# Messages in 25 tiles of 128 nodes, one P add in four on VectorE, key one-hots on ScalarE, and the second update ahead in the last stage of a two-layer graph network

## The chip, the cores and the metric

The kernel runs on 1 core of one Trainium2 chip. The metric is the device time of one execution in microseconds (us). Short names for the engines are those of the profile: PE (TensorE, with PEld for its weight loads), DVE (VectorE), ACT (ScalarE), POOL (GpSimd) and SP (SyncE, which only issues transfers).

## The reference, cut to what matters

There are 3,125 nodes with 256 features and 50,000 edges sorted by their destination. Layer 0 is a max-pooling graph layer. Layer 1, which this change touches, is an attention layer:

```python
h = relu(layernorm(x))
e = edge_emb[edge_type]                       # 16 types
messages = (h[src] + e) @ msg_W + msg_b
att_in = concat([h[src], h[dst], e, task_rep])
edge_delta = tanh(gelu(att_in @ att_W1 + att_b1) @ att_W2 + att_b2)
edge_weight = 1.0 + edge_scale * edge_delta
messages = (messages * (1 + 0.5 * tanh(msg_gamma)) + msg_beta) * edge_weight
agg = segment_sum(messages, dst) / max(segment_sum(edge_weight, dst), 1)
agg = agg * (1 + 0.5 * tanh(upd_gamma)) + upd_beta
updated = gelu(concat([h, agg]) @ up_W1 + up_b1) @ up_W2 + up_b2
y = h + updated
x = x + layernorm(y) * ln_g + ln_b
```

## The kernel before

The nodes are cut into 28 windows of 112 (WIN), taken four at a time (GN = 4) as 7 node groups (NG). The edges, sorted by destination, are put into 418 slots of up to 128 edges, so that a slot's destinations lie in one window; four slots (SG) are one edge group, which gives 105 edge groups (NGR), the last with 2 slots. The program has three parts that matter here; all orders are written out by hand, engine by engine, with semaphores between the engines.

**Node stage.** For each node group PE turns the rows of h (`turn_h`, L1397), DVE copies the result from PSUM into `up` (L1709), and `messages` (L1409) multiplies it by two weight matrices of 256 columns each. That gives per node a row of 512 numbers: P (256, the source's part of the attention input) and M (256, the message without edge weight). One message tile is the 112 nodes of one window, with 4 matmuls; ACT and DVE take turns in copying it out (`take`), and SP writes it to `pm_d` in HBM. `neigh` (L1386) and `keys_q` (L1422) are other products of the same stage; `keys_q` makes Q, the destination's part, which is kept in three bf16 pieces in `qw`.

**Edge stage.** `edge_step(g)` is run by every engine for each edge group g. POOL gathers the rows [P, M] of the four slots from `pm_d` (L1353), six groups of buffers round. PE (L1490, L1492) builds z of a slot in PSUM: three bf16 matmuls with the key one-hot `hot` (which edge belongs to which node of the window, and to which type) as weights and the three pieces of Q as data, and one fp32 matmul with the identity that adds the gathered P. Slots 0 and 1 lie in one PSUM bank, 2 and 3 in the next, and groups take turns between two pairs of banks. ACT applies Gelu to each bank (L1596). DVE multiplies by the attention vector and sums to a logit (L1763). One step later ACT makes the edge weight from it (tanh L1608, scale L1610) and scales the placement one-hots `place` (L1615); two steps after z PE sums the messages with them into windows (L1516, banks 4 to 7), and three steps after z DVE adds these sums into `acc` (L1750). DVE also makes the one-hots: types and placement (L1753, L1754), and the keys of the group after (`match_keys(g + 1)`, L1727). `hot` has two buffers. In 9 of the 105 groups (`pair_of`) PE also multiplies a pair of windows by the first half of `up_W1` (L1503), and ACT puts the result back into `up` (L1602).

**Last stage.** Per node group: ACT makes a diagonal of 1/degree, PE multiplies the aggregates with it (`update`, L1874), DVE adds the node's own part (`update`, L1956), ACT applies Gelu (L1935), PE multiplies by `up_W2` (`rows_y`, L1884), DVE adds h and takes the statistics (`rows_y`, L1966 to L1977), POOL takes the root (L1847), DVE makes the shift (`shifts`, L1982), ACT normalizes (L1922), and DVE multiplies and adds (`put`, L1990, L1993). PE's `update(i)` waits until DVE has read what `update(i - 1)` left in the bank:

```python
for f in range(2):
    if i >= 1:
        eng.wait_ge(u_ready, 2 * i - 1 + f)
```

Of the kernel before, what the change touches and what calls it, by code (L numbers as in the profile page):

```python
# [6 lines left out]
def gnn_two_layers(nc, A, out):  # L7
# [8 lines left out]
    P = 128  # L16
# [60 lines left out]
    with top:  # L77
# [1072 lines left out]
        with b34:  # L1150
# [12 lines left out]
            pm = [gbuf[0:WIN, r * GN * 2 * D:(r + 1) * GN * 2 * D] for r in range(2)]  # L1163
# [8 lines left out]
            onec = cols[:, 0:1]  # L1172
            ramp = bank(7)[:, AW:AW + P]
# [41 lines left out]
            hot_ready = sem("hot_ready")  # L1215
            z_ready = sem("z_ready")
            gelu_ready = sem("gelu_ready")
# [48 lines left out]
            def pm_parts(i):  # L1266
                return [(0, GN)] if i < NG - 1 else [(0, 2), (2, 3), (3, 4)]
# [7 lines left out]
            def _(eng):  # L1275
# [6 lines left out]
                for i in range(NG):  # L1282
# [3 lines left out]
                    for k0, k1 in pm_parts(i):  # L1286
                        eng.wait_ge(pm_a, 2 * i + (k1 + 1) // 2)
                        eng.wait_ge(pm_v, 2 * i + k1 // 2)
                        rows = slice((i * GN + k0) * WIN, (i * GN + k1) * WIN)
                        eng.dma_start(pm_d[rows, :].rearrange("(k p) d -> p k d", p=WIN), rows_by_k(pm[i % 2])[:, k0:k1, :])\  # L1290
                           .then_inc(pm_out[i % 2], 16)
# [66 lines left out]
            def _(eng):  # L1358
# [31 lines left out]
                def turn_h(i):  # L1390
                    eng.wait_ge(h_ready, i + 1)
                    if i >= 1:
                        eng.wait_ge(pm_a, 2 * i - 1)
                        eng.wait_ge(pm_v, 2 * i - 1)
# [18 lines left out]
                def keys_q(i):  # L1413
# [5 lines left out]
                    for k in range(GN):  # L1419
                        at = (i * GN + k) * ACW0  # L1420
                        for hf in range(2):
                            ins = eng.matmul(q_bank(i)[0:WIN, k * D:(k + 1) * D], up[:, at + hf * WIN:at + (hf + 1) * WIN],  # L1422
# [24 lines left out]
                for i in range(NG):  # L1447
# [5 lines left out]
                    messages(i, range(GN))  # L1453
# [5 lines left out]
                def own_early(p):  # L1459
                    if p == 0:  # L1460
                        eng.wait_ge(pm_a, 2 * NG)
                        eng.wait_ge(pm_v, 2 * NG)
                    if p >= 3:
                        eng.wait_ge(u_out, p - 2)
                    for f in range(2):
                        for hf in range(2):
                            ins = eng.matmul(early_bank(p)[:, f * ACW0:(f + 1) * ACW0], upw1[:, hf * D + f * P:hf * D + (f + 1) * P],
                                             pair_cols(p)[:, :, hf, :], start=hf == 0, stop=hf == 1)
# [10 lines left out]
                def edge_step(g, r, n):  # L1479
                    if has(g):  # L1480
# [17 lines left out]
                    if p is not None:  # L1498
                        eng.wait_ge(logit_ready, g)
                        for f in range(2):  # L1500
                            to = bank(2 * ((g + 1) % 2))[:, f * ACW0:(f + 1) * ACW0]
                            for hf in range(2):
                                ins = eng.matmul(to, upw1[:, hf * D + f * P:hf * D + (f + 1) * P],  # L1503
                                                 pair_cols(p)[:, :, hf, :], start=hf == 0, stop=hf == 1)
                        ins.then_inc(u_ready, 1)
                    if has(g - 2):
# [16 lines left out]
            def _(eng):  # L1523
# [16 lines left out]
                def take(i, k):  # L1540
                    if k == 0 and i >= 2:
                        eng.wait_ge(pm_out[i % 2], 16 * (i // 2))
                    eng.wait_ge(pm_ready, GN * i + k + 1)
                    eng.activation(pm[i % 2][:, k * 2 * D:(k + 1) * 2 * D], bank(4 + k)[0:WIN, :], ACT.Copy).then_inc(pm_a, 1)
# [486 lines left out]
```

## Time and profile before

| | us |
|---|---|
| median of 3 runs (1302.63 to 1306.84) | 1305.84 |
| the profiled execution's own time | 1307.77 |
| its span, from the first to the last instruction | 1305.8 |
| PE busy, share of the span | 937.8 (72%) |
| DVE busy | 899.9 (69%) |
| POOL busy | 831.5 (64%) |
| ACT busy | 605.0 (46%) |

The span contains both layers. The node stage begins near 551 us, PE's first matmul of the edge stage is at 700.65 us, and the last stage begins at 1230.8 us. A share of the whole span is a mean over stages with different limits, so each stage has to be read by itself, from the rows of its own stretch of time.

### The profile page before, as it was taken

To read this page: it belongs to the slowest core of one execution; us is meant where nothing else is said; L and a number is where in the kernel's file an instruction comes from. 1 tells how busy PE (TensorE), PEld (TensorE's weight loads), DVE (VectorE), ACT (ScalarE), POOL (GpSimd) and SP (SyncE) were. 2 spreads that over 40 slices of the span, in tenths; PEclk is the share of its full clock that TensorE was granted. 3 is DMA by queue.
4 is the path that set the end of the run, shared out by engine and by line. 5 is a ranking of instruction groups with operands and counts; after the bars stand their busy time and mean duration, and the time that the engine had idled before them with its cause. 6 is when DMAs were issued, how large, how long until landed. Compare 5 with 4: busy or idle time off the path is not lost. (4 is left out here: it accounts for less than half of the span.)

```text
span 1305.8 us, 18685 instructions
## 1 busy us (share of the span) xinstructions
PE 937.8 (72%) x5019; PEld 728.9 (56%) x5019; DVE 899.9 (69%) x2594; ACT 605.0 (46%) x1479; POOL 831.5 (64%) x868
## 2 busy tenths in 40 slices
PE   7505455664123511389899999999999999999985
PEld 6402233332112510277677777777777777777774
DVE  6477575665566544345656888888888888888658
ACT  6433333433243433223325665566666656556544
POOL 0377777777777777663127777777777777777012
PEclk9855555555555555589899999999999999999988
DMA  5568666566776666544357777877877787887312
GB/s 157 133 201 279 220 214 216 201 224 221 241 261 232 201 204 216 191 116 130 69 152 231 235 234 235 241 235 234 238 239 236 232 236 241 234 235 237 99 38 85
DMA packets 100774, 263.58 MB, mean 202 GB/s; under 512 B 21094, under 2 KB 42117, under 8 KB 94530
## 3 DMA queue, kind: packets, MB, share of 16 engines
q0 software_dynamic: 53856, 164.87, 42.7%
q1 hardware_dynamic: 45026, 95.76, 22.1%
q10 hardware_dynamic: 1792, 1.75, 0.5%
q8 instruction: 46, 0.75, 0.2%
q14 instruction: 54, 0.44, 0.1%
HBM read 192.92 MB, written 68.25 MB: 200 GB/s over the span
## 5 line engine op out<-in xcount | busy, mean ns | idle before, releaser
L675 POOL DMA_INDIRECT gath<-hp_d,chain_src x391 | 370.8, 948 | 169.3 <-issue 166.3
L1353 POOL DMA_INDIRECT gbuf<-pm_d,srcs x350 | 332.1, 949 | 108.5 <-issue 104.1
L922 DVE SCALAR_TENSOR_TENSOR hist<-hist,smask,ps 128x256 f32<-128x256 f32 x390 | 186.7, 479 | 194.8 <-ACT ps L716 186.8
L716 ACT ACTIVATE ps<-gath,chain_w 128x256 f32<-128x256 f32 x391 | 164.6, 464 | 312.9 <-DMA gath<-hp_d,chain_src 295.1
L1750 DVE TENSOR_TENSOR acc<-ps,acc 112x272 f32 x418 | 183.7, 439 | 69.2 <-DVE acc L1750 64.0
L1596 ACT ACTIVATE ps<-ps 128x512 f32<-128x512 f32 x210 | 122.1, 582 | 191.7 <-PE ps L1492 191.6
L1492 PE MATMUL ps<-gbuf,ident 128*128 128x256 f32 x700 | 210.1, 382 | 0.0
L1490 PE MATMUL ps<-qw,halves 128*128 x1254 | 206.6, 274 | 2.3 <-DVE qw L1699 2.3
L1516 PE MATMUL ps<-gbuf,placed 128*112 128x272 f32 x700 | 175.4, 393 | 1.0 <-ACT placed L1615 0.7
L837 PE MATMUL ps<-win_hot,node_hot 128*112 128x28 bf16 x391 | 43.7, 253 | 175.2 <-DVE win_hot L1009 175.2
L1490 PEld LDWEIGHTS ps<-qw,halves 128*128 128x128 bf16 x1254 | 122.9, 98 | 73.8 <-issue 6.9
L1516 PEld LDWEIGHTS ps<-gbuf,placed 128*112 128x112 f32 x700 | 123.4, 177 | 35.2 <-ACT placed L1615 1.2
L837 PEld LDWEIGHTS ps<-win_hot,node_hot 128*112 128x112 bf16 x391 | 40.0, 207 | 181.2 <-DVE win_hot L1009 179.8
L1763 DVE CUSTOM_DVE_ANT_0 gbuf<-ps,w2b 128x256 f32<-128x256 f32 x350 | 127.6, 417 | 8.6 <-ACT ps L1596 8.6
L1615 ACT ACTIVATE placed<-placed,logit 128x112 f32<-128x112 f32 x418 | 128.0, 376 | 3.4
L1492 PEld LDWEIGHTS ps<-gbuf,ident 128*128 128x128 f32 x700 | 106.4, 192 | 3.9
L761 PE MATMUL ps<-wsT,hT_s 128*112 128x256 f32 x112 | 57.2, 666 | 50.7 <-ACT hT_s L723 40.4
L1353 POOL DMA_INDIRECT attw<-pm_d,srcs x68 | 64.3, 946 | 21.1 <-issue 20.4
L761 PEld LDWEIGHTS ps<-wsT,hT_s 128*112 128x112 f32 x112 | 30.1, 299 | 71.8 <-issue 54.9
L1754 DVE TENSOR_TENSOR placed<-ps,edgef 128x448 f32<-128x448 f32 x105 | 64.4, 613 | 0.0
L1847 POOL TENSOR_TENSOR rs_c<-ve_c,power 112x4 f32<-112x4 f32 x7 | 12.5, 1789 | 77.1 <-DVE ve_c L1977 77.1
L1007 DVE TENSOR_TENSOR node_hot<-ps,low 128x896 bf16<-128x896 f32 (+1 forms) x49 | 52.9, 1080 | 0.0
(292 smaller groups left out, 1384.2 us busy)
## 6 DMA issues: line engine op xcount, KB each, us to landing
hist_d<-hist SPq DMA_DIRECT2D x48, 1024.0 KB, 4.6
gath<-hp_d,chain_src POOLq DMA_INDIRECT x391, 3.1
wn<-node_row_d SPq DMA_DIRECT2D x26, 224.0 KB
key<-node_row_d SPq DMA_DIRECT2D x26, 224.0 KB, 3.5
gbuf<-pm_d,srcs POOLq DMA_INDIRECT x350, 4.0
pm_d<-gbuf SPq DMA_DIRECT2D x6, 896.0 KB, 5.1
hb_d<-gbuf SPq DMA_DIRECT2D x7, 448.0 KB, 3.2
qw<-hb_d SPq DMA_DIRECT2D x7, 448.0 KB, 8.4
```

Source lines behind the costliest of these rows:

```text
L675: eng.indirect_dma_start(row_at(j), None, hp_d[:, :], bass.IndirectOffsetOnAxis(ap=chain_src[:, j:j + 1], axis=0)).then_inc(got[q % RINGG] ...
L716: eng.activation(weighted_at(j), row_at(j), ACT.Copy, scale=chain_w[:, j:j + 1]).then_inc(gw_ready, 1)
L761: ins = eng.matmul(bank(6, 2)[0:WIN, k * D:(k + 1) * D], hT[i % 2][:, (k * 2 + hf) * WIN:(k * 2 + hf + 1) * WIN], wsT[:, hf * D:(hf + 1) * ...
L922: eng.scalar_tensor_tensor(out=state_at(j), in0=state_at(j - 1) if j else first_state[:, :], scalar=smask[:, j:j + 1], in1=weighted_at(j), ...
L1353: eng.indirect_dma_start(gath3(g % RING)[:, k, 0:2 * D], None, pm_d[:, :], bass.IndirectOffsetOnAxis(ap=srcs[:, g * SG + k:g * SG + k + 1] ...
L1490: eng.matmul(to, hot[g % 2][:, k * P:(k + 1) * P], qw[:, bass.ds(w[k] * (3 * D) + part * D, D)], start=part == 0, stop=False)
L1492: ins = eng.matmul(to, ident[:, :], gath3(r)[:, k, 0:D], start=False, stop=True)
L1516: eng.matmul(bank(4 + k)[0:WIN, 0:AW], place[q % 3][:, k * WIN:(k + 1) * WIN], gath3(q)[:, k, D:SW], start=True, stop=True).then_inc(sums_ ...
L1596: eng.activation(zb, zb, ACT.Gelu).then_inc(gelu_ready, 1)
L1615: ins = eng.activation(at, at, ACT.Copy, scale=logit[q][:, k:k + 1])
L1750: eng.tensor_tensor(to, bank(4 + k)[0:WIN, 0:AW], to, ALU.add).then_inc(summed, 1)
L1763: ins = eng.tensor_tensor_reduce(gath3(r)[:, k, 0:D], zk, w2b[:, :], 1.0, 0.0, ALU.mult, ALU.add, logit[r % 3][:, k:k + 1])
```

## The change

Four edits, in one file:

1. Message tiles are 128 nodes wide: 25 tiles (the last of 64 nodes) instead of 28 of 112. For this `up` is laid out as two halves of 3,136 columns, so that 128 neighbouring nodes are neighbouring columns; DVE's copy of the turned rows is two instructions of 128x448 instead of one of 128x896. A node group completes 3, 4, 3, 4, 3, 4 and 4 tiles.
2. For the fourth slot of each full edge group PE leaves out the fp32 matmul with the identity, and DVE adds P into PSUM (semaphore `p_added`). ACT's second Gelu of the group waits for it.
3. `match_keys` moves from DVE to ACT and becomes two passes: |key - p| in place with ACT's Abs and the bias `less` = -p, then relu(1 - that) into `hot`. PE's wait for `hot_ready` ahead of the fourth placement matmul is dropped.
4. In the last stage DVE runs `update(1)` ahead of `rows_y(0)` and `shifts(0)`.

```diff
-            def pair_cols(p):
-                return up[:, p * 2 * ACW0:(p + 1) * 2 * ACW0].rearrange("p (k h n) -> p k h n", k=2, h=2)
+            def nodes(n0, n1, half):
+                return up[:, half * NT * WIN + n0:half * NT * WIN + n1]
+
+            def pair_cols(p, half):
+                return nodes(p * 2 * WIN, (p + 1) * 2 * WIN, half).rearrange("p (k n) -> p k n", k=2)
...
+            def tiles_of(i):
+                first, last = i * GN * WIN // P, (i + 1) * GN * WIN // P
+                return range(first, last if i < NG - 1 else -(-NM // P))
+
+            def nodes_in(m):
+                return min(P, NM - m * P)
...
+            def p_by_vector(g, k):
+                return slots_in(g) == SG and k == SG - 1
...
-                def messages(i, ks):
...
-                    for k in ks:
-                        if i >= 1 and k >= 2:
-                            eng.wait_ge(pm_a if k == 2 else pm_v, 2 * i)
-                        at = (i * GN + k) * ACW0
+                    for k, m in enumerate(tiles_of(i)):
+                        if i >= 1 and k == 2:
+                            eng.wait_ge(pm_a, by_act(i))
+                        if i >= 1 and k == 3:
+                            eng.wait_ge(pm_v, by_vec(i))
+                        n = nodes_in(m)
                         for half, w in enumerate((attw[:, 0:2 * D], mc[:, :])):
                             for hf in range(2):
-                                ins = eng.matmul(bank(4 + k)[0:WIN, half * D:(half + 1) * D], up[:, at + hf * WIN:at + (hf + 1) * WIN],
+                                ins = eng.matmul(bank(4 + k)[0:n, half * D:(half + 1) * D], nodes(m * P, m * P + n, hf),
                                                  w[:, hf * D:(hf + 1) * D], start=hf == 0, stop=hf == 1)
                         ins.then_inc(pm_ready, 1)
...
                         for k in range(slots_in(g)):
                             to = bank(2 * (g % 2), 2)[:, k * D:(k + 1) * D]
                             for part in range(3):
-                                eng.matmul(to, hot[g % 2][:, k * P:(k + 1) * P],
-                                           qw[:, bass.ds(w[k] * (3 * D) + part * D, D)], start=part == 0, stop=False)
-                            ins = eng.matmul(to, ident[:, :], gath3(r)[:, k, 0:D], start=False, stop=True)
+                                ins = eng.matmul(to, hot[g % 2][:, k * P:(k + 1) * P],
+                                           qw[:, bass.ds(w[k] * (3 * D) + part * D, D)], start=part == 0,
+                                           stop=part == 2 and p_by_vector(g, k))
+                            if not p_by_vector(g, k):
+                                ins = eng.matmul(to, ident[:, :], gath3(r)[:, k, 0:D], start=False, stop=True)
                             if k == slots_in(g) - 1:
                                 ins.then_inc(z_ready, 2 - k // 2)
...
                             if k == SG - 1:
                                 eng.wait_ge(match_ready, min(g + 1, NGR))
-                                eng.wait_ge(hot_ready, min(g + 2, NGR))
                             eng.matmul(bank(4 + k)[0:WIN, 0:AW], place[q % 3][:, k * WIN:(k + 1) * WIN],
...
+                eng.wait_ge(one_set, 2)
+
+                def match_keys(g):
+                    n, at = g // KG, g % KG * GW
+                    key_g = key[n % 2][:, at:at + GW]
+                    eng.wait_ge(key_in[n % 2], (n // 2 + 1) * 32)
+                    eng.activation(key_g, key_g, ACT.Abs, bias=less[:, 0:1]).then_inc(apart, 1)
+                    eng.wait_ge(apart, g + 1)
+                    eng.activation(hot[g % 2], key_g, ACT.Relu, scale=-1.0, bias=onec).then_inc(hot_ready, 1)
+
+                match_keys(0)
...
                 def edge_step(g, r, n):
                     if has(g):
                         for half in range(2):
                             eng.wait_ge(z_ready, g * 2 + half + 1)
+                            if half == 1 and slots_in(g) == SG:
+                                eng.wait_ge(p_added, g + 1)
                             zb = bank(2 * (g % 2) + half)
                             eng.activation(zb, zb, ACT.Gelu).then_inc(gelu_ready, 1)
+                    if has(g + 1):
+                        match_keys(g + 1)
...
                     eng.wait_ge(t_ready, i + 1)
-                    eng.tensor_copy(up[:, i * GN * ACW0:(i + 1) * GN * ACW0].rearrange("p (k c) -> p k c", k=GN),
-                                    bank(4, 2).rearrange("p (k c) -> p k c", k=GN)[:, :, 0:ACW0]).then_inc(hT_ready, 1)
+                    for hf in range(2):
+                        ins = eng.tensor_copy(nodes(i * GN * WIN, (i + 1) * GN * WIN, hf).rearrange("p (k n) -> p k n", k=GN),
+                                              bank(4, 2).rearrange("p (k c) -> p k c", k=GN)[:, :, hf * WIN:(hf + 1) * WIN])
+                    ins.then_inc(hT_ready, 1)
...
-                    if has(g + 1):
-                        match_keys(g + 1)
+                    if has(g) and slots_in(g) == SG:
+                        eng.wait_ge(z_ready, g * 2 + 2)
+                        zk = bank(2 * (g % 2), 2)[:, (SG - 1) * D:SG * D]
+                        eng.tensor_tensor(zk, zk, gath3(r)[:, SG - 1, 0:D], ALU.add).then_inc(p_added, 1)
...
                 update(0)
+                update(1)
                 rows_y(0)
                 shifts(0)
-                update(1)
```

On ACT, the second edge group in the loop, before (L1596 Gelu, L1608 and L1610 the edge weight of the group before, L1615 its placement one-hots):

```order
L1596 ACTIVATE ps<-ps 128x512 [waits z_ready] x2
L1608 ACTIVATE logit1<-logit1,b2c 128x4 [waits logit_ready]
L1610 ACTIVATE logit1<-logit1,cols,esc 128x4 [waits delta_ready]
L1615 ACTIVATE placed<-placed,logit1 128x112 [waits match_ready,ew_ready]
L1615 ACTIVATE placed<-placed,logit1 128x112 x3
```

The same group's rows after the change (L1639 Gelu, L1624 Abs, L1626 Relu, which gives `hot_ready`):

```order
L1639 ACTIVATE ps<-ps 128x512 [waits z_ready]
L1639 ACTIVATE ps<-ps 128x512 [waits p_added,z_ready]
L1624 ACTIVATE key<-key,less 128x512 [waits key_in1]
L1626 ACTIVATE halves<-key,cols 128x512 [waits apart]
L1653 ACTIVATE logit1<-logit1,b2c 128x4 [waits logit_ready]
L1655 ACTIVATE logit1<-logit1,cols,esc 128x4 [waits delta_ready]
L1660 ACTIVATE placed<-placed,logit1 128x112 [waits match_ready,ew_ready]
L1660 ACTIVATE placed<-placed,logit1 128x112 x3
```

The keys of group g + 1 stand behind the second Gelu of group g, and that Gelu now waits for DVE as well as for PE.

On DVE, one edge group before, from the one-hots to the logits (L1753, L1754 types and placement, L1727 keys, L1763 logits):

```order
L1753 TENSOR_TENSOR gbuf<-ps,edgef 128x4x16
L1754 TENSOR_TENSOR placed<-ps,edgef 128x448
L1727 TENSOR_TENSOR halves<-key,ps 128x512 [waits key_in1]
L1763 ISA gbuf,logit1<-ps,w2b 128x256 [waits gelu_ready]
L1763 ISA logit1 128x1
```

After (L1798, L1799 types and placement, L1804 the P add, L1810 logits):

```order
L1798 TENSOR_TENSOR gbuf<-ps,edgef 128x4x16
L1799 TENSOR_TENSOR placed<-ps,edgef 128x448
L1804 TENSOR_TENSOR ps<-ps,gbuf 128x256 [waits z_ready]
L1810 ISA gbuf,logit0<-ps,w2b 128x256 [waits gelu_ready]
L1810 ISA logit0 128x1
```

The keys are gone from between the one-hots and the logits, and the P add, which waits until PE has made the whole group's z, stands in their place.

On DVE, the start of the last stage before (L1956 `update`, L1966 `rows_y`, L1982 `shifts`; semaphore names are shared with an earlier block):

```order
L1956 TENSOR_TENSOR u0<-ps,up 128x448 [waits x_in5] x2
L1966 TENSOR_TENSOR y_c0<-ps,qw 112x1024 [waits bias_in,hb_in0]
...
L1982 SCALAR_TENSOR_TENSOR nb_c<-mv_c,rs_c 112x4 [waits io_read]
L1956 TENSOR_TENSOR u1<-ps,up 128x448 [waits x_in5] x2
L1956 TENSOR_TENSOR u0<-ps,up 128x448 [waits x_in5,bias_in]
```

After (L2003 `update`, L2013 `rows_y`, L2029 `shifts`):

```order
L2003 TENSOR_TENSOR u0<-ps,up 128x448 [waits wp_in] x2
L2003 TENSOR_TENSOR u1<-ps,up 128x448 [waits wp_in] x2
L2013 TENSOR_TENSOR y_c0<-ps,qw 112x1024 [waits io_set,hb_in0]
...
L2029 SCALAR_TENSOR_TENSOR nb_c<-mv_c,rs_c 112x4 [waits wT_ready]
L2003 TENSOR_TENSOR u0<-ps,up 128x448 [waits wp_in,io_set]
```

The two adds of `update(1)` (u1) have moved ahead of the statistics of the first group.

## Rows read from the trace of the kernel before

**Rows 1.** Busy time by engine, edge stage: from, to, length, engines, clock, DMA.
```profile
700.65:1220.35 519.70, 519.70 (x2969) 405.57 (x2970) 443.51 (x1545) 313.76 (x842) 382.91 (x406) 1.00 0.78 232
```

**Rows 2.** Timeline of PE in one edge group: start, us, instruction, count.
```profile
904.91 0.49 PE L1490 MATMUL ps<-qw,halves 128*128 x3
905.24 0.60 PE L1492 MATMUL ps<-attw,ident 128*128 128x256 f32 x2
...
907.20 0.49 PE L1490 MATMUL ps<-qw,halves 128*128 x3
...
907.96 2.00 PE L1516 MATMUL ps<-gbuf,placed 128*112 128x272 f32 x8
...
909.79 0.49 PE L1490 MATMUL ps<-qw,halves 128*128 x3
```

**Rows 3.** Timeline of ACT in the same edge group.
```profile
908.16 0.58 ACT L1596 ACTIVATE ps<-ps 128x512 f32<-128x512 f32 x1 [0.94 <-PE ps L1492]
...
908.65 0.29 ACT L1608 ACTIVATE logit<-logit,b2c 128x4 f32<-128x4 f32 x1
...
908.98 0.39 ACT L1610 ACTIVATE logit<-logit,cols,esc 128x4 f32<-128x4 f32 x1
...
909.40 1.22 ACT L1615 ACTIVATE placed<-placed,logit 128x112 f32<-128x112 f32 x4
```

**Rows 4.** Timeline of DVE in the same edge group.
```profile
904.59 0.44 DVE L1750 TENSOR_TENSOR acc<-ps,acc 112x272 f32 x1
...
907.03 0.61 DVE L1754 TENSOR_TENSOR placed<-ps,edgef 128x448 f32<-128x448 f32 x1
907.56 0.68 DVE L1727 TENSOR_TENSOR halves<-key,ps 128x512 bf16<-128x512 bf16 x1
...
908.16 0.41 DVE L1763 CUSTOM_DVE_ANT_0 attw<-ps,w2b 128x256 f32<-128x256 f32 x1
...
909.53 0.43 DVE L1750 TENSOR_TENSOR acc<-ps,acc 112x272 f32 x1
```

**Rows 5.** ACT's groups by line and shape: busy us, mean ns, idle before.
```profile
L1608 ACT ACTIVATE logit<-logit,b2c 128x4 f32<-128x4 f32 x105 | 30.3, 288 | 0.0
...
L246 ACT ACTIVATE sd<-ve 112x4 f32<-112x4 f32 x7 | 1.4, 194 | 3.0 <-DVE ve L345 2.9
...
L269 ACT ACTIVATE hpo<-hpb 112x512 f32<-112x512 f32 x2 | 1.3, 629 | 1.1 <-DVE hpb L370 1.0
```

**Rows 6.** POOL's gathers in the edge stage, timeline.
```profile
905.47 0.94 POOL L1353 DMA_INDIRECT gbuf<-pm_d,srcs  x1 [0.30 <-issue]
```

**Rows 7.** Timeline of the node stage, message tiles of two node groups.
```profile
643.94 2.05 PE L1409 MATMUL ps<-attw,up 128*112 128x256 f32 x4 [1.67 <-DVE up L1709]
...
658.16 1.09 DVE L1709 COPY up<-ps 128x896 f32<-128x896 f32 x1 [3.53 <-PE ps L1397]
...
659.30 1.12 PE L1409 MATMUL ps<-attw,up 128*112 128x256 f32 x4 [1.19 <-DVE up L1709]
```

**Rows 8.** The chain that ended last, in the last stage, in order of time.
```profile
1241.86 3.47 PE ps L1884 x16
...
1249.87 0.16 DVE nb_c L1982
1250.03 0.55 DVE u L1956
...
1250.71 3.73 PE ps L1874 x16
...
1260.29 1.24 DVE y_c L1966
...
1266.72 2.01 PE ps L1874 x16
1268.73 0.89 PE ps L1862 x8
1269.62 3.12 PE ps L1884 x15
```

More of the change, by code:

```diff
@@ L1162, in gnn_two_layers @@
             gath = [gbuf[:, r * SG * SW:(r + 1) * SG * SW] for r in range(RING - 1)] + [attw[:, :]]
-            pm = [gbuf[0:WIN, r * GN * 2 * D:(r + 1) * GN * 2 * D] for r in range(2)]
+            pm = [gbuf[:, r * GN * 2 * D:(r + 1) * GN * 2 * D] for r in range(2)]
             h, hb, ngb = ([gbuf[0:WIN, (4 + 2 * n + r) * GN * D:(5 + 2 * n + r) * GN * D] for r in range(2)] for n in range(3))
@@ L1172, in gnn_two_layers @@
             onec = cols[:, 0:1]
+            less = s("less", [P, 1], fp32)
             ramp = bank(7)[:, AW:AW + P]
@@ L1238, in early_bank, with by_act, by_vec @@
                 return bank(4 + p % 3)
-            def pair_cols(p):
-                return up[:, p * 2 * ACW0:(p + 1) * 2 * ACW0].rearrange("p (k h n) -> p k h n", k=2, h=2)
+            def nodes(n0, n1, half):
+                return up[:, half * NT * WIN + n0:half * NT * WIN + n1]
+            def pair_cols(p, half):
+                return nodes(p * 2 * WIN, (p + 1) * 2 * WIN, half).rearrange("p (k n) -> p k n", k=2)
+            NM = NT * WIN
+            def tiles_of(i):
[3 more added lines that the diff above has]
+                return min(P, NM - m * P)
+            def by_act(i):
+                return sum((len(tiles_of(n)) + 1) // 2 for n in range(i))
+            def by_vec(i):
+                return sum(len(tiles_of(n)) // 2 for n in range(i))
             def slots_in(g):
                 return min(SG, USED - g * SG)
+            def p_by_vector(g, k):
+                return slots_in(g) == SG and k == SG - 1
             def gath3(r):
@@ L1266, in pm_parts @@
             def pm_parts(i):
-                return [(0, GN)] if i < NG - 1 else [(0, 2), (2, 3), (3, 4)]
+                return [(0, len(tiles_of(i)))] if i < NG - 1 else [(0, 2), (2, 3), (3, 4)]
+            assert len(tiles_of(NG - 1)) == GN and max(len(tiles_of(i)) for i in range(NG)) <= GN
             def put_all(eng):
@@ L1286, in _ @@
                     for k0, k1 in pm_parts(i):
[L1287 to L1291, printed above, removed]
+                        eng.wait_ge(pm_a, by_act(i) + (k1 + 1) // 2)
+                        eng.wait_ge(pm_v, by_vec(i) + k1 // 2)
+                        m0, m1 = tiles_of(i)[k0], tiles_of(i)[k1 - 1] + 1
+                        n = nodes_in(m1 - 1)
+                        eng.dma_start(pm_d[m0 * P:(m1 - 1) * P + n, :].rearrange("(k p) d -> p k d", p=n),
+                                      rows_by_k(pm[i % 2])[0:n, k0:k1, :]).then_inc(pm_out[i % 2], 16)
                     if i == REC_AT:
@@ L1452, in _ @@
                         turn_n(i + 2)
-                    messages(i, range(GN))
+                    messages(i)
                     if i + 2 < NG:
@@ L1467, in own_early @@
                             ins = eng.matmul(early_bank(p)[:, f * ACW0:(f + 1) * ACW0], upw1[:, hf * D + f * P:hf * D + (f + 1) * P],
-                                             pair_cols(p)[:, :, hf, :], start=hf == 0, stop=hf == 1)
+                                             pair_cols(p, hf), start=hf == 0, stop=hf == 1)
                     ins.then_inc(u_ready, 1)
@@ L1503, in edge_step @@
                                 ins = eng.matmul(to, upw1[:, hf * D + f * P:hf * D + (f + 1) * P],
-                                                 pair_cols(p)[:, :, hf, :], start=hf == 0, stop=hf == 1)
+                                                 pair_cols(p, hf), start=hf == 0, stop=hf == 1)
                         ins.then_inc(u_ready, 1)
@@ L1542, in take @@
                         eng.wait_ge(pm_out[i % 2], 16 * (i // 2))
-                    eng.wait_ge(pm_ready, GN * i + k + 1)
-                    eng.activation(pm[i % 2][:, k * 2 * D:(k + 1) * 2 * D], bank(4 + k)[0:WIN, :], ACT.Copy).then_inc(pm_a, 1)
+                    m = tiles_of(i)[k]
+                    n = nodes_in(m)
+                    eng.wait_ge(pm_ready, m + 1)
+                    eng.activation(pm[i % 2][0:n, k * 2 * D:(k + 1) * 2 * D], bank(4 + k)[0:n, :], ACT.Copy).then_inc(pm_a, 1)
                 def q_high(i):
@@ L1621, in _ @@
                 eng.memset(onec, 1.0).then_inc(one_set, 1)
+                eng.tensor_scalar(less[:, :], pcol[:, 0:1], -1.0, None, ALU.mult).then_inc(one_set, 1)
                 def merge():
```

47 lines of the change are left out of this document (23 added, 24 removed).

## The prediction

> **What bounds the kernel now.** I cut the span into stages with the view of busy time by stretches, and the edge stage is 519.7 of 1305.8 us [rows 1]. In it PE is busy all the time at full clock (2.4 GHz), DVE 443.5 us, ACT 313.8 us. So this is where most of the change acts, and I read one edge group there in the timeline, engine by engine.
>
> PE's group starts at 904.91 and the next at 909.79: 4.88 us [rows 2]. Four slots of z take the first part: a slot is three bf16 matmuls (0.33 to the start of the fp32 one) and the fp32 P matmul; from 904.91 to 907.20 are three slots, 0.763 each, so the P matmul is 0.43. The four placement matmuls with their split passes take from 907.96 to 909.79, 1.83. Nothing is left over: 4 x 0.763 + 1.83 = 4.88.
>
> Two other engines are close behind. DVE starts its first accumulation at 904.59 and the next group's at 909.53, 4.94, with no long idle [rows 4]. POOL needs 0.94 + 0.31 = 1.25 for a gather, 5.0 for the four of a group [rows 6]; it stays in step because its ring was filled ahead and because PE has extra matmuls in 9 groups. So a PE that needs less than 4.88 would gain little by itself: POOL's 418 gathers at 1.25 are 522 us, as long as the stage.
>
> In the last stage the chain of waits shows a hole: PE's `rows_y(0)` ends at 1241.86 + 3.47 = 1245.33, and its next matmul starts at 1250.71, because it waits for DVE's `update(1)`, which stands behind the statistics and the shift of group 0 [rows 8].
>
> **The change, part by part.**
>
> *P add and keys together.* PE's own work per group falls by the P matmul to 4.45. But two things that were independent are now in series. Before, the keys of group g + 1 were made by DVE ahead of the logits of group g, while PE was still in z(g). After, they stand on ACT behind the second Gelu of g, that Gelu waits for DVE's P add, and the P add waits for the last z of g. PE can't start z(g + 1) without these keys. Buffers don't help, since the maker of the keys never gets more than one group ahead. The loop, counted from PE's first matmul of z(g):
>
> - to the end of the last bf16 trio and the hand-over to DVE: 907.20 - 904.91 = 2.29, + 0.49 + 0.03 = 2.81 [rows 2]. (The 0.03 is the distance at which Gelu follows in the same way: 907.20 + 0.33 + 0.60 of the P matmuls = 908.13, Gelu at 908.16 [rows 3].)
> - P add, 128x256 from PSUM: not in the trace. Nearest are the accumulation of 112x272 from PSUM at 0.44 and the multiply of 128x256 at 0.41 [rows 4]; I take 0.42, plus 0.03 hand-over: 3.26.
> - second Gelu until the next ACT instruction can start: 908.16 to 908.65, 0.49 [rows 3]: 3.75.
> - Abs of 128x512 with a bias column. ACT on 512 columns without such an operand takes 0.629; a bias column adds 0.288 - 0.194 = 0.09 (tanh of 4 columns with it against the root of 4 columns without) [rows 5]. So 0.72, and a dependent ACT instruction starts 0.04 after its source ends (908.65 + 0.29 to 908.98) [rows 3]: 4.51.
> - Relu of the same size, also with a bias column: 0.72: 5.23.
> - hand-over to PE: 0.13 lie between the end of DVE's u (1250.03 + 0.55) and PE's matmul at 1250.71 [rows 8]; here a register instruction stands between, so I take 0.2: 5.43.
>
> Group time 5.43 against 4.88 is +0.55. There are 105 groups, so 104 steps from one to the next, 9 of them with the pair's matmuls; in those PE is busy with the pair while ACT makes the keys, and I count them as even. 95 x 0.55 = **+52 us**. The others have room in 5.43: ACT has 2 x 0.49 for Gelu, 0.65 + 0.76 for the keys, 0.33 + 0.42 + 1.22 for weights and placement [rows 3], 4.36 in all; DVE 4.94 - 0.60 (keys, 907.56 to 908.16) + 0.35 + about 0.1 of waiting for Gelu, 4.8 [rows 4]; POOL 5.0.
>
> The bounds. An Abs or Relu can't be shorter than the Gelu of the same size, 0.58 [rows 3]: loop 5.15, +26. bf16 input on ACT isn't in the trace. Upwards, two passes of 0.77 and 0.3 for the hand-over give 5.63, +71. The middle value is nearest to its rows, since only a pointer operand is added to the 512-column row.
>
> The Trainium skill, "ScalarE: Activation LUTs", section "What ACT_TABLE_LOAD costs", gives about 280 ns + 0.833 ns per column for an ACTIVATE with a bias pointer, fp32 and bf16 alike: 0.71 for 512 columns, by which the term would be an estimated +50. Its 186 ns without the pointer agrees with the 194 ns of the 4-column root [rows 5]. No row here shows the bf16 half of it; if it failed, the faster rival below would gain.
>
> *Dropped wait on the keys ahead of the fourth placement matmul*: 0. DVE's keys came at 907.56 + 0.68 and that matmul starts after 909.3.
>
> *25 tiles.* A message tile has four fp32 matmuls of 256 columns, the form of the P matmul at 0.43 [rows 2], so 1.72. Three tiles fewer are -5.2. PE is in the path there: its message matmuls run through and neighbour and key products follow at once. DVE's copy ahead of them, 1.09 [rows 7], becomes two of 448 columns, about 0.53 + 0.61 as for the placement one-hots of 448 columns (907.03 to 907.56, lasting 0.61) [rows 4], +0.06 to 0.1 for each of 7 groups, +0.6. Saved copies and writes are beside PE. Sum **-4.6**; between 0, if a DVE-paced step swallows it, and -7, since at 643.94 four matmuls took 2.05 instead of 1.12 after an idle 1.67 and one of the saved tiles is of that group.
>
> *First keys on ACT*: about 1.4 on ACT near 698, done with DVE's last Q piece; 0, or +1.
>
> *Second update ahead.* PE goes on at 1245.4 with `update(2)`, turned types and `rows_y(1)`: 2.01 + 0.89 + 3.12 = 6.0, as in a later group at full clock. So y(1) can start near 1251.45 instead of 1260.29 [rows 8]. DVE's shift at 1249.87, 0.16, and `update(2)`, 0.55 + 0.6, end at 1251.2, just in time. This is **-8.8**: 5.4 of hole, and the rest because PE came back at half clock (1.2 GHz: 3.73 for what later takes 2.01). After it DVE sets a pace of its own that stays. Bounds: -5.4, if PE drops in clock all the same, and -9.5.
>
> Sum: +52 - 4.6 - 8.8 = +39. The profiled execution took 1307.8 with a span of 1305.8; it is 2 us, 0.15%, over the median of 1305.84. Span 1345, and by the median **1345 us**.
>
> **The rivals.**
>
> *A, forecast: the key loop paces the edge stage*, group time 5.3 to 5.65. Chance 0.77.
>
> *B, the same loop, milder*: passes near Gelu's 0.58, group time 5.1 to 5.3, time 1314 to 1332 (95 x 0.22 - 13.4 = +7.5; 95 x 0.42 - 13.4 = +26.5). 0.10.
>
> *C, the loop doesn't bind, and the kernel is faster.* The passes on ACT would be so short that key time hides behind PE's 1.83 of placement. It decides where the loop falls under 4.88 + 13.4 / 95 = 5.02, that is each pass at 0.51 instead of 0.72. Against it: the shortest pass over 512 columns here is Gelu's 0.58 [rows 3]. With it, POOL's 5.0 and DVE's 4.8 take over, the stage ends 3 to 6 us earlier, and the time is 1305.8 - 13.4 - 5 = 1287. 0.06; within 0.3% there is 0.03 between B and C.
>
> *D, PE loses its clock.* It now idles 5.43 - 4.45 = 1 us in each group. For it: after 1.67 idle at 643.94 the clock was half; against it: after 1.19 idle at 659.30 the four matmuls took 1.12, full speed [rows 7]. If it ran at half clock in a quarter of the groups, z would take 2.6 more there: 26 x 2.6 = +68, time near 1413. 0.04. The Trainium skill, "TensorE: Matmul & The Clock Gate", section "HAM oscillation — how this bites in real kernels", tells of kernels in which idle gaps in every round of a loop bring the clock down again and again; 659.30 doesn't show it, 643.94 does.
>
> **The numbers.** Likeliest 1345. The range takes in A with its bounds (T of 5.2 to 5.63: 95 x 0.32 - 13.4 = +17, 95 x 0.75 - 13.4 = +58) and half of B: 1317 to 1364. About 0.3% (4 us) is what a measurement of this kernel can tell from no change. Slower than that: A + B + most of D = 0.91; same 0.03; faster 0.06.
>
> **What would show it.** In the changed profile: PE's group time 5.4, with one idle of about 1 us ahead of z's first matmul, released by ACT's Relu (L1626); PE's busy share in the edge stage 82%; Abs and Relu at 0.72 each; DVE idle before the P add (L1804), released by PE; POOL waiting for PE's sums, as its ring runs full; the last stage 8 to 9 us shorter, with no half clock near 1250; the node stage 4 to 5 shorter. It is wrong if Abs or Relu is well under 0.6, if PE's first matmul of a group waits for something else (a gather, DVE's logits), or if PE is at half clock in the edge stage.

## The result, and the profile after

The changed kernel takes 1362.43 us (median of 4 runs, 1361.37 to 1363.88), the kernel before 1305.73 us beside it (4 runs, 1302.63 to 1306.84). The ratio is 1.0439 with a 95% interval of 1.0419 to 1.0459: slower, 17 us above the predicted 1345. The profiled execution took 1362.09, its span is 1360.3. In three of the five sets of experiments the kernel before, run beside them, took 1532 to 1545 us; those experiments are given as ratios alone, at the end of their section, and no size is taken from them.

I cut the span as before. The node stage, the edge stage and the last stage of the changed kernel, in the view of busy time by stretches (from, to, length, then PE, PEld, DVE, ACT, POOL, clock, DMA share, GB/s; the first stretch begins 1.5 us after the node stage does):

```profile
550.75:694.65 143.90, 125.46 (x634) 105.41 (x634) 76.74 (x144) 45.91 (x72) 61.46 (x54) 0.96 0.47 133
694.65:1284.05 589.40, 500.04 (x2761) 361.28 (x2761) 435.66 (x1548) 452.17 (x1051) 381.89 (x405) 0.99 0.69 204
1293.89:1360.30 66.41, 50.33 (x320) 43.73 (x320) 48.85 (x111) 33.94 (x77) 12.52 (x7) 0.90 0.39 98
```

The edge stage, from PE's first z to the first matmul of the last group, took 519.7 us and now takes 589.4 [rows 1]. PE's busy time there fell from 519.7 to 500.0: it has less to do, and is idle for 89 us (589.4 - 500.0). ACT's rose by 138 us. The clock is 0.99 in the mean, so over the stage as a whole little is lost to it; its start is another matter, below. The bounds of the stages give this account:

| stretch | before | after | difference | forecast |
|---|---|---|---|---|
| start to node stage | 550.8 | 549.2 | -1.6 | 0 |
| node stage, to the first z | 149.9 | 145.4 | -4.5 | -4.6 |
| edge stage | 519.7 | 589.4 | +69.7 | +52 |
| end of the edge stage | 10.4 | 9.8 | -0.6 | 0 |
| last stage | 75.0 | 66.4 | -8.6 | -8.8 |
| span | 1305.8 | 1360.3 | +54.5 | +39 |

(The first row is the part of the program that the change doesn't touch; in the traces of the five experiments told one by one below it ends between 549.6 and 552.4, so its -1.6, and the -0.6, are scatter that happened to fall on the side of a smaller miss.)

One turn of the edge loop in the changed kernel, the last full one, in the timeline (start, us, instruction; in brackets the idle time before it and what the trace names for it):

```profile
1278.51 0.53 PE L1518 MATMUL ps<-qw,halves 128*128 x3 [0.89 <-DVE logit L1810]
...
1280.83 0.49 PE L1518 MATMUL ps<-qw,halves 128*128 x3
...
1281.16 2.00 PE L1545 MATMUL ps<-attw,placed 128*112 128x272 f32 x8
1281.36 0.43 DVE L1804 TENSOR_TENSOR ps<-ps,gbuf 128x256 f32<-128x256 f32 x1 [0.65 <-PE ps L1518]
...
1281.89 0.58 ACT L1639 ACTIVATE ps<-ps 128x512 f32<-128x512 f32 x1 [1.03 <-DVE ps L1804]
...
1282.38 0.71 ACT L1624 ACTIVATE wn<-wn,less 128x512 bf16<-128x512 bf16 x1
...
1283.12 0.72 ACT L1626 ACTIVATE halves<-wn,cols 128x512 bf16<-128x512 bf16 x1
...
1284.05 0.53 PE L1518 MATMUL ps<-qw,halves 128*128 x3 [0.89 <-DVE logit L1810]
```

Read it as a staircase: each row starts just after the one above it has given its result, across three engines, and the last is the first instruction of the next turn. 5.54 us a turn, where PE's own work set 4.88 [rows 2]. The steps from the last trio to the end of the Relu are the same to 0.01 us in every turn of the stage; from turn to turn only PE's z (2.31 to 2.48 at full clock) and the last step to PE (0.20 to 0.29, where there is no pair) vary. The placement matmuls end at 1283.16, and PE stands for 0.89 us. The trace puts that wait down to DVE's logits, L1810. But the logits that z of the next group needs are those of the group before this one, and they had ended a group earlier; the Relu of the keys ended at 1283.84, 0.21 before the matmul. A wait for several semaphores is named after one of them, and here the name misleads. At the stage's start it doesn't: z of the second group waits for no logits yet, and there the row names the Relu, 0.14 after its end. The same timeline, from the first group's Relu on:

```profile
700.94 0.72 ACT L1626 ACTIVATE halves<-wn,cols 128x512 bf16<-128x512 bf16 x1
...
701.80 0.82 PE L1518 MATMUL ps<-qw,halves 128*128 x3 [2.66 <-ACT halves L1626]
...
703.27 0.85 PE L1518 MATMUL ps<-qw,halves 128*128 x3
...
708.95 0.82 PE L1518 MATMUL ps<-qw,halves 128*128 x3 [2.72 <-DVE logit L1810]
```

The first two turns take 7.15 us and the third 6.98, not 5.54. The first two have no placement matmuls yet, so PE stands for 2.7 us behind each, and after such a wait the first two trios of a z take 0.82 to 0.85 where they take 0.49 later: half clock. The view of busy time over the first three turns shows it, with a granted clock of 0.76. The second row is the kernel before over its first three turns, with 0.87:

```profile
694.65:715.93 21.28, 15.00 (x62) 10.12 (x63) 7.54 (x33) 10.80 (x23) 10.19 (x12) 0.76 0.53 160
700.65:713.35 12.70, 12.70 (x69) 9.48 (x69) 7.85 (x32) 6.19 (x16) 9.57 (x11) 0.87 0.77 237
```

The kernel before needed 12.70 us from its first z to that of the fourth group. So the 69.7 us of the edge stage are: 21.28 - 12.70 = 8.6 in the first three turns; 83 ordinary turns that took 4.88 us in the mean and now take 5.56 (5.54 in most, up to 5.70), 56.3; and 4.8 in the nine turns with a pair and the nine behind them, which took 6.41 + 4.88 and now take 6.24 + 5.59.

The waits of the edge stage, by engine and line (us in total, times, longest), and ACT's two key passes by line and shape:

```profile
ACT ps L1639 <- DVE ps L1804: 107.1, 103, 1.4
PE ps L1518 <- DVE logit L1810: 85.2, 93, 2.7
POOL gbuf L1379 <- PE ps L1545: 83.4, 76, 8.0
...
DVE ps L1804 <- PE ps L1518: 76.5, 102, 4.5
```
```profile
L1626 ACT ACTIVATE halves<-wn,cols 128x512 bf16<-128x512 bf16 x53 | 38.2, 722 | 1.7
L1624 ACT ACTIVATE wn<-wn,less 128x512 bf16<-128x512 bf16 x53 | 37.7, 712 | 0.0
```

PE, DVE and ACT now stand in nearly every group, and POOL in most: no engine is the bound, the circle of PE, DVE and ACT is, and POOL stands behind it.

In the last stage of the changed kernel, PE, DVE and the shift of two groups:

```profile
1304.81 3.62 PE L1931 MATMUL ps<-upw,u 128*112 128x256 f32 x16
...
1308.27 1.94 PE L1921 MATMUL ps<-dg,acc 128*128 128x112 f32 x16
1308.54 1.23 DVE L2013 TENSOR_TENSOR y_c<-ps,qw 112x1024 f32<-112x1024 f32 x1 [3.79 <-PE ps L1931]
...
1314.66 1.22 DVE L2013 TENSOR_TENSOR y_c<-ps,qw 112x1024 f32<-112x1024 f32 x1 [0.43 <-PE ps L1931]
```

PE goes from one group's `rows_y` to the `update` of a later group without a pause, and its 16 records take 1.94 us where they took 3.73 after the hole [rows 8]. From y(0) to y(1) are 6.12 us.

### The profile page after: what moved, and what is told of

Its sections match the earlier page's. It is cut to its first block and busy times, and to the rows that moved or that the text cites. A ratio compares the mean times of both kernels' runs of the same rounds, so it can differ in the third digit from the quotient of the medians.

```text
span 1360.3 us, 18537 instructions
## 1 busy us (share of the span) xinstructions
PE 904.9 (67%) x4787; PEld 675.5 (50%) x4787; DVE 889.2 (65%) x2597; ACT 744.4 (55%) x1689; POOL 829.5 (61%) x868
## 5 line engine op out<-in xcount | busy, mean ns | idle before, releaser
L1518 PE MATMUL ps<-qw,halves 128*128 x1254 | 213.7, 277 | 91.7 <-DVE logit L1810 86.1
L1639 ACT ACTIVATE ps<-ps 128x512 f32<-128x512 f32 x210 | 122.1, 582 | 127.2 <-DVE ps L1804 108.1
L1522 PE MATMUL ps<-gbuf,ident 128*128 128x256 f32 x526 | 160.1, 387 | 0.0
L1810 DVE CUSTOM_DVE_ANT_0 gbuf<-ps,w2b 128x256 f32<-128x256 f32 x350 | 133.7, 420 | 2.9 <-ACT ps L1639 0.2
L1545 PEld LDWEIGHTS ps<-gbuf,placed 128*112 128x112 f32 x700 | 118.7, 177 | 30.1 <-ACT placed L1660 1.8
L1804 DVE TENSOR_TENSOR ps<-ps,gbuf 128x256 f32<-128x256 f32 x87 | 37.6, 433 | 70.1 <-PE ps L1518 70.1
L1522 PEld LDWEIGHTS ps<-gbuf,ident 128*128 128x128 f32 x526 | 81.9, 196 | 2.4
L1799 DVE TENSOR_TENSOR placed<-ps,edgef 128x448 f32<-128x448 f32 x105 | 64.5, 614 | 0.0
```

The lines of the kernel that those rows point to most:

```text
L1518: ins = eng.matmul(to, hot[g % 2][:, k * P:(k + 1) * P], qw[:, bass.ds(w[k] * (3 * D) + part * D, D)], start=part == 0, stop=part == 2 and ...
L1545: eng.matmul(bank(4 + k)[0:WIN, 0:AW], place[q % 3][:, k * WIN:(k + 1) * WIN], gath3(q)[:, k, D:SW], start=True, stop=True).then_inc(sums_ ...
L1639: eng.activation(zb, zb, ACT.Gelu).then_inc(gelu_ready, 1)
L1810: ins = eng.tensor_tensor_reduce(gath3(r)[:, k, 0:D], zk, w2b[:, :], 1.0, 0.0, ALU.mult, ALU.add, logit[r % 3][:, k:k + 1])
```

## The experiments

Theory 1: the place of the keys on ACT, behind the second Gelu and only one group ahead, closes the loop; the work itself does not cost the time. Theory 2: ACT's two passes, or the P add on DVE, cost it by their length wherever they stand. Four kernels take the change apart, with all else as in the changed kernel, and a fifth changes the distance alone.

**The keys of g + 1 ahead of both Gelus.** Same instructions, same engines, another order on ACT; the keys no longer wait for the P add.

```diff
 def edge_step(g, r, n):                # ACT
+    if has(g + 1):
+        match_keys(g + 1)
     if has(g):
         ... both Gelus ...
-    if has(g + 1):
-        match_keys(g + 1)
```

> The changed kernel with one move: ScalarE makes the keys of group g + 1 ahead of both Gelus of group g. Work on every engine is the same as after the change. Theory 1 (the keys stand in series behind the P add and the second Gelu): the loop through the keys is gone, nothing is slower than GpSimd's 5.0 us a group, the edge stage from PE's first z to its last takes 508 to 516 us instead of 589, time 1281 to 1290, faster than the kernel before. Rival 2 (ScalarE has simply too much to do, or slows the others by its traffic): time stays near 1362. Rival 3 (VectorE with the P add is the next bound, at 5.2 or more a group): 541 us or more for the edge stage, time 1313 or more.

Measured: 1288.22 us (4 runs, 1286.5 to 1289.7) against 1305.35 of the kernel before (7 runs), ratio 0.9863 (0.9841 to 0.9884). It is 1.4% faster than the kernel before and 74 us below the changed one, by the place of two instructions. The edge stage takes 512.1 us up to the last z trio. One group in its timeline:

```profile
905.11 0.71 ACT L1624 ACTIVATE wn<-wn,less 128x512 bf16<-128x512 bf16 x1
...
905.84 0.72 ACT L1626 ACTIVATE halves<-wn,cols 128x512 bf16<-128x512 bf16 x1
...
906.49 0.61 DVE L1799 TENSOR_TENSOR placed<-ps,edgef 128x448 f32<-128x448 f32 x1
907.02 0.42 DVE L1804 TENSOR_TENSOR ps<-ps,gbuf 128x256 f32<-128x256 f32 x1
...
907.54 0.58 ACT L1641 ACTIVATE ps<-ps 128x512 f32<-128x512 f32 x1 [0.49 <-DVE ps L1804]
...
908.88 0.53 PE L1518 MATMUL ps<-qw,halves 128*128 x3 [0.95 <-DMA gbuf<-pm_d,srcs]
```

The keys are ready at 906.56, long before PE wants them at 908.88. The P add follows the placement one-hots with no idle time, so up to here DVE is the one that runs through: 4.80 us a group in its rows. But PE here waits for a gather. The waits of its edge stage:

```profile
POOL gbuf L1379 <- issue: 99.3, 326, 0.3
...
PE ps L1518 <- DMA gbuf<-pm_d,srcs: 13.8, 19, 1.9
DVE ps L1804 <- PE ps L1518: 12.1, 13, 4.6
...
PE ps L1518 <- DVE logit L1810: 2.8, 5, 1.2
POOL gbuf L1379 <- PE ps L1545: 2.8, 8, 0.6
```

The three waits of the circle fell from 85.2, 83.4 and 76.5 us to 2.8, 2.8 and 12.1. POOL, which stood for PE, now stands almost only for its own issuing, 0.3 us a gather. Theory 1 holds, theory 2 falls.

The new pace changes hands within the stage. Ahead of 905 us PE waits once for a gather, for 0.2 us; behind it, in the waits from 905 to 1208 us, PE's longest and all of POOL's into these buffers are:

```profile
PE ps L1518 <- DMA gbuf<-pm_d,srcs: 13.6, 18, 1.9
POOL gbuf L1379 <- issue: 60.3, 198, 0.3
```

POOL had issued the last gather of a group 12.7 us before PE's first z of it at the start of the stage, and only 3 to 4 us before from the middle on. From the 44th group to the last a turn takes (1207.78 - 903.07) / 61 = 5.00 us, which is POOL's four gathers of 1.25. So in the second half POOL's gathers set the pace, and no longer DVE.

**P add back on PE, keys left behind the Gelus.**

```diff
 def p_by_vector(g, k):
-    return slots_in(g) == SG and k == SG - 1
+    return False
```

(with the wait on `p_added` and DVE's add taken out).

> The changed kernel with the fourth P add back on PE; the keys stay on ScalarE behind the second Gelu. Theory 1: the P matmul's 0.43 us takes the place of the P add with its hand-overs (0.43 + 0.09), so the loop through the keys stays, 5.4 to 5.5 us a group, time 1346 to 1358: the keys' place costs nearly everything, and the P add on VectorE 5 to 15 us. Rival 3 (the P add on VectorE is what costs): back to 4.9 a group, time near 1292.

Measured: 1357.47 us in one run, edge stage 583.1 us up to the last z trio, where the changed kernel has 590.2 and the kernel before 520.5. So the loop without the P add costs nearly all. Its group in the timeline:

```profile
904.37 0.49 PE L1518 MATMUL ps<-qw,halves 128*128 x3
...
905.33 0.58 ACT L1637 ACTIVATE ps<-ps 128x512 f32<-128x512 f32 x1 [0.94 <-PE ps L1522]
905.83 0.71 ACT L1624 ACTIVATE wn<-wn,less 128x512 bf16<-128x512 bf16 x1
...
906.57 0.72 ACT L1626 ACTIVATE halves<-wn,cols 128x512 bf16<-128x512 bf16 x1
...
907.49 0.53 PE L1518 MATMUL ps<-qw,halves 128*128 x3 [0.36 <-issue]
```

From the last trio to the Gelu are 0.96 us over PE's P matmul; over DVE they are 1281.89 - 1280.83 = 1.06. The add on DVE makes the loop 0.10 longer, 5.54 against 5.44. This comes from the rows; a difference of 5 us between the times, with one run here, would not carry it alone.

**Keys back on DVE, P add on DVE.** The opposite half.

```diff
 def match_keys(g):                     # DVE, ahead of the P add
-    eng.activation(key_g, key_g, ACT.Abs, bias=less[:, 0:1])
-    eng.activation(hot[g % 2], key_g, ACT.Relu, scale=-1.0, bias=onec)
+    eng.tensor_tensor(hot[g % 2], key_g, pnum.to_broadcast([P, GW]), ALU.is_equal)
```

(and the wait on the keys ahead of the fourth placement matmul is back).

> The changed kernel with the keys back on VectorE at their old place, as one compare; the fourth P add stays on VectorE. Theory 1: the loop through the keys is gone, but VectorE now has the P add on top of a list that was already as long as PE's, 5.3 to 5.4 us a group, time 1325 to 1336. Rival 2 (ScalarE's load is the cause): ScalarE is back to its old list, time near 1285 to 1292.

Measured: 1331.66 us in one run, a group 5.39 us, but in another way. DVE and PE in the timeline:

```profile
898.41 0.61 DVE L1796 TENSOR_TENSOR placed<-ps,edgef 128x448 f32<-128x448 f32 x1
898.94 0.68 DVE L1771 TENSOR_TENSOR halves<-key,ps 128x512 bf16<-128x512 bf16 x1
899.54 0.42 DVE L1803 TENSOR_TENSOR ps<-ps,gbuf 128x256 f32<-128x256 f32 x1
...
899.76 0.68 PE L1546 MATMUL ps<-gbuf,placed 128*112 128x272 f32 x2 [0.55 <-DVE halves L1771]
```

The five kinds of work on DVE stand back to back, with no idle time but the 0.21 between accumulations, and now PE waits for DVE's keys. Moving the P add to DVE without taking the keys off it makes DVE the bound: 104 x 5.39 = 561, and from its first z to that of the last group are 558.4 us. Rival 2, ScalarE's load, falls here too: ScalarE has its old list back, and the kernel is still 26 us slower than the one before.

**The edge stage as before, tiles and second update as changed.**

> The kernel before with only the 25 tiles and the second update ahead (both edits of the edge stage undone). The traces put the tiles and what lies ahead of the edge stage at -6.0 us and the last stage at -8.6 us. If these two are what they seem, 1290 to 1293. If PE, once it reaches the edge stage earlier, only waits for gathers there, 1296 or more.

Measured: 1295.34 us (4 runs, 1295.05 to 1296.54), ratio 0.9915 (0.9894 to 0.9936), 2.3 us above the upper end of what was expected. In its trace the node stage takes 145.6 us, the edge stage 519.2 up to the last z trio (before 520.5), the last stage 66.4. The two parts are worth 4.3 + 8.6 = 12.9 us, for 13.4 in the forecast; against that the untouched first part ended 1.7 us later in this trace. The 1.3 us by which the edge stage is shorter come from its start. PE's first z came after 2.35 us of idle time as in the kernel before (2.34), but here it ran at full clock, and the first three turns, the same work, took 11.06 us instead of 12.70:

```profile
698.05:709.11 11.06, 11.06 (x69) 8.48 (x69) 7.85 (x32) 6.19 (x16) 8.31 (x10) 1.00 0.76 232
```

**The keys in their place behind the Gelus, but two groups ahead.** If the loop is the cause, a distance of two groups should free it with the order on ACT unchanged.

```diff
+match_keys(1)                          # beside match_keys(0), before the loop
...
     both Gelus of g
-    if has(g + 1):
-        match_keys(g + 1)
+    if has(g + 2):
+        match_keys(g + 2)
```

> Keys behind the second Gelu, made two groups ahead, once more at another time. Where the kernel before takes 1305 us: theory 1 (what costs is that z of g + 1 needs what stands behind the Gelu of g) 1283 to 1291 us and 4.8 to 5.0 us a group; rival (the place itself costs) above 1310.

Measured: 1288.53 us (4 runs, 1286.99 to 1289.85) against 1305.97, ratio 0.9865 (0.9842 to 0.9889). The Abs still follows the second Gelu, and the waits of the circle are gone; from its timeline and its waits:

```profile
902.06 0.58 ACT L1640 ACTIVATE ps<-ps 128x512 f32<-128x512 f32 x1 [0.49 <-DVE ps L1805]
...
902.55 0.71 ACT L1624 ACTIVATE key<-key,less 128x512 bf16<-128x512 bf16 x1
```
```profile
DVE ps L1805 <- PE ps L1518: 17.2, 11, 4.5
PE ps L1518 <- issue: 5.8, 9, 0.9
POOL gbuf L1379 <- PE ps L1545: 5.5, 15, 1.2
```

So it is the distance, not the place as such: the same instruction in the same place is nearly free when what it makes is wanted a group later. Not quite free: in the nine turns with a pair PE waits for ACT's scaled one-hots, which stand behind the keys, 4.7 us in all, and these turns take 6.6 to 7.0 us.

**The experiments given as ratios alone.** First the two-ahead kernel, in the two runs before the one above.

> The changed kernel with the keys at their place behind the second Gelu, but made two groups ahead instead of one (keys of g + 2 behind the Gelus of g; groups 0 and 1 are made before the loop). Theory 1: what costs is that z of g + 1 needs what stands behind the Gelu of g; with the keys a group earlier the loop spans two groups and binds no more, edge stage 508 to 516 us, time 1283 to 1291, as with the keys ahead of the Gelus. Rival (the place itself costs, since it holds ACT between the Gelu and the edge weights and delays these): 5.2 a group or more, time above 1310.

> The same kernel as in the run before (keys behind the second Gelu, two groups ahead), again, since the kernel before itself took 1532 us there and every engine had stalls of several us without a releaser. In groups without such a stall that trace has 4.80 to 5.0 us a group, so theory 1 expects, where the kernel before takes 1305, 1283 to 1291 us; the rival (the place behind the Gelu itself costs) above 1310.

Ratios 1.0169 (1.0114 to 1.0225) and 1.0053 (1.0014 to 1.0092), unlike the 0.9865 above. No cause is shown for the difference, and I draw nothing from the ratios of the next two kernels beyond a sign.

> Keys on ScalarE ahead of both Gelus, and the fourth P add back on PE: the changed kernel with the loop gone and without the P add on VectorE. Theory 1: PE's own 4.88 us a group binds again, though VectorE has 0.6 us less than before; time 1293 to 1297, like the kernel with both edits of the edge stage undone (1295.3). If VectorE had been a bound of the kernel before beside PE, it would be under 1290.

> The same kernel as before (keys on ScalarE ahead of the Gelus, P add on PE), again for the same reason. Theory 1: PE's 4.88 a group binds, 1293 to 1297 us; if VectorE had been a bound of the kernel before beside PE, under 1290.

> Keys on ScalarE ahead of both Gelus, the fourth P add back on PE, once more at another time. Where the kernel before takes 1305 us: theory 1, PE's own 4.88 us a group binds, edge stage 517 to 521 us and time 1293 to 1297, as with both edits of the edge stage undone (1295.3); the P add on VectorE is then worth about 7 us once the keys are out of the loop (1288.2 with it). If VectorE had been a bound of the kernel before beside PE, under 1290, and the P add would be worth nothing.

Keys first, P add on PE: 0.9855 (0.9803 to 0.9906), 0.9825 (0.9761 to 0.9888) and 0.9876 (0.983 to 0.9921). In none of the three traces is a turn of the edge stage shorter than 4.88 us, while with the P add on DVE and the loop broken turns go down to 4.45. That fits the step from 1295.3 (edge stage undone) to 1288.2 (keys first), which holds both moves. What the P add on DVE alone gains once the loop is gone stays open.

> The kernel before with only the 25 message tiles (second update at its old place). The stretch from PE's first matmul of the node stage to its first z should take 145 to 146 us instead of 149.9, and nothing else should change: time 1301 to 1304, ratio to before 0.996 to 0.999; the last stage 75.0 us as before, against 66.4 with the second update ahead.

> The same kernel as before (only the 25 message tiles), again for the same reason: time 1301 to 1304, ratio to before 0.996 to 0.999, last stage 75.0 us.

Tiles alone: 0.9957 (0.9923 to 0.999) and 0.996 (0.9932 to 0.9989). The sign agrees with the node stage in the traces of the five kernels above; those carry the size.

## Why the prediction was right, and where its size was off

Slower, by the mechanism of forecast A. The time is 17 us above the value named and only 1.6 us inside the upper end of the range, 1364.

**The key loop** was right as a mechanism, and shown by four kernels: the changed one, the two in which it is broken, each its own way, both at 1288, and the one without the P add on DVE, where it stays, at 1357. Its size was low: 5.54 instead of 5.43 a group. Step by step, as the prediction counted it:

| step | forecast | measured |
|---|---|---|
| PE's z, first to last trio | 2.29 | 2.32 |
| trio to P add | 0.52 | 0.53 |
| P add to Gelu | 0.45 | 0.53 |
| Gelu to Abs | 0.49 | 0.49 |
| Abs to Relu | 0.76 | 0.74 |
| Relu to PE's next z | 0.92 | 0.93 |
| sum | 5.43 | 5.54 |

The first mis-sized term is the turn itself, 83 x (0.68 - 0.55) = 11 us. About half of it, 83 x 0.07 = 6 us, is the hand-over from the P add to the Gelu: I took 0.03 us, the distance at which a Gelu follows PE; after DVE's add it is 1281.36 + 0.43 to 1281.89, 0.10. Most of the rest is PE's z, which is 0.03 longer when its first trio comes after a wait (0.53 for 0.49), and 0.02 more in the mean over the turns.

The second is the start of the stage, which I priced like any turn, 3 x 0.55 = 1.7 us, and which cost 8.6. Two things were missed there. Before, a turn without placement matmuls was short (the second group's z started 4.73 behind the first, the third's 3.05 behind that); the loop has no such turns, since all of its steps are there from the first group on. At full clock this is 3 x 5.54 - 11.06 = 5.6, with the 11.06 us of the kernel whose edge stage is undone. The half clock cost 21.28 - 3 x 5.54 = 4.7, and 12.70 - 11.06 = 1.6 of that the kernel before had as well, so 3.0 came new. 11 + 7 = 18 is the whole miss of this term, 17.4, within its rounding. The pairs came out even: counted as nine turns at 0 and the nine behind them at 0.55, 5.0, they came to 4.8, since the turns with a pair became 0.17 shorter and those behind them 0.71 longer.

**The two passes** at 0.72 were right: 0.712 for Abs, 0.722 for Relu, so rival B (passes near 0.58) falls. The Trainium skill, "ScalarE: Activation LUTs", section "What ACT_TABLE_LOAD costs", gives 280 ns and 0.833 ns per column with a bias pointer, in bf16 as in fp32, by which 512 columns are an estimated 0.71; the trace agrees, now for bf16 too.

**Rival C**, the loop doesn't bind: it would have needed passes of 0.51. But its price was close. With the loop broken the kernel takes 1288.2 and 1288.5, and C said 1287. What then paces it is what C named, both of it: with the keys first, DVE's 4.80 a group, and from the 44th group on POOL's 5.0. The stage is 511 us long and not the 522 of 418 gathers at 1.25, because 14 of them were issued ahead of it.

**Rival D**, the clock: wrong for the loop, right for its first turns. With 0.9 us idle in each turn of 5.54 the granted clock is 0.99 over the stage; with 2.7 us idle in a turn of 7.15 it was half for most of a z. I had priced it for a quarter of the groups and set it against the forecast as a whole; it came as a small part of the edge stage, 4.7 us, of which the kernel before had 1.6. In the node stage the half clock is where it was before the change, behind an idle time of 1.74:

```profile
640.29 2.07 PE L1437 MATMUL ps<-attw,up 128*128 128x256 f32 x4 [1.74 <-DVE up L1760]
```

The Trainium skill, "TensorE: Matmul & The Clock Gate", section "HAM oscillation — how this bites in real kernels", warns of idle gaps in every round of a loop; in this kernel z ran at half clock at first behind gaps of 2.35, 2.66 and 2.72 us, and never behind the gaps of 0.9 us in the hundred turns after them. The length of the gap alone doesn't decide it: with the edge stage undone z ran at full clock behind 2.35 us.

**Dropped wait, first keys:** forecast at 0; no run takes either by itself, and nothing in the rows speaks against it. **25 tiles:** -4.5 against -4.6, and part of this closeness is luck: the first eight matmul records of the stage took 3.57 us before and 1.95 after, half clock against full, which is 1.6 of the 4.5. The five kernels above, with the same tiles, give -3.6 to -6.8 for the node stage, four of them -3.6 to -4.3. **Second update:** -8.6 against -8.8, and in the traces of the same five the last stage is 65.7 to 66.4 us long.

**The signs named ahead.** Seen: the idle time ahead of z, passes of 0.72, DVE waiting for z ahead of the P add (0.65), POOL waiting for PE's sums, and no half clock in the `update` that came after the hole. PE's busy share is 500.0 of 589.4, 85% for the forecast 82%; the view counts the last placement matmul to its own end, 2.00 us for the eight records, where the next matmul could start after 1.83 [rows 2]. Not as written: the trace names DVE's logits ahead of z, not ACT's Relu, and by the letter "waits for DVE's logits" was listed as a sign against me. The row at 701.80, the end of the Relu 0.2 to 0.3 us ahead of each z that has no pair before it, and the two kernels that break the loop settle it the other way.

## What to carry to other kernels

When work moves from one in-order engine to another, its length matters less than what now stands ahead of it there, and how many rounds ahead its result is made. Follow one round from an instruction to its own next turn, through every engine: if the sum is above the busiest engine's time, that is the time of the round. Then ask whether the producer can stand ahead of the wait, or run one round further ahead. Here either one turned a kernel 4.4% slower into one 1.4% faster than the one before. And ask what paces the stage once the loop is gone: an engine that only waited in the slow kernel can be next in line, as POOL was.

## What the runs showed of the hardware

- A Gelu that follows DVE's add to PSUM starts 0.10 us after it ends; behind PE's matmul it starts after 0.03 [rows 2, 3].
- From the end of ACT's Relu to PE's matmul are 0.20 us in most turns of two kernels, and up to 0.29.
- At the start of the stage z ran at half clock behind idle times of 2.35 to 2.72 us (granted clock 0.76 over three turns), and at full clock behind 0.9. In the kernel with the edge stage undone z ran at full clock behind 2.35 (1.00 over three turns).
- A P add on DVE (0.43) is no shorter in the path than the fp32 matmul that it replaces: 1.06 us from the last trio to the Gelu against 0.96.
- POOL's gathers of 128 rows follow each other at 1.25 us (0.95 and 0.30 of issue), in the keys-first kernel from 905 us on without waiting for anyone, and four of them, 5.00 us, are then the time of a turn.
